# Second attention of a two-layer stack: from whole chunks of 128 tokens to two halves of 64 with a state between them

## What is computed

```python
def step(carry, qkv):
    S_K, C_QV, G = carry
    q_t, k_t, v_t = qkv
    C_prev = GAMMA * C_QV
    k_C = einsum('bhk,bhkv->bhv', k_t, C_prev)
    G = GAMMA * G + k_t[..., :, None] * k_C[..., None, :]
    S_K = GAMMA * S_K + k_t[..., :, None] * k_t[..., None, :]
    C_QV = C_prev + q_t[..., :, None] * v_t[..., None, :]
    S_C = einsum('bhij,bhjv->bhiv', S_K, C_QV)
    o_t = einsum('bhk,bhkv->bhv', q_t, S_C - G)
    return (S_K, C_QV, G), o_t
out = outs @ Wo
```

## Time and profile before

| what | value |
|---|---|
| median of 3 runs | 700.54 us |
| lowest, highest | 699.94, 701.98 us |
| span of the profiled execution, first to last instruction | 697.8 us |
| PE busy over the span | 640.0 us, 92% |
| DVE, ACT, POOL busy | 421.9, 301.7, 254.2 us |
| mean granted TensorE clock, share of full speed | 0.956 |

### The profile page before, as it was taken

The page is one execution under the profiler, slowest core; times in us unless marked ns, Lnnn a source line. Parts: engine busy times, 40 slices in busy tenths (PEclk is TensorE's granted clock), DMA queues, the critical chain, the costliest instruction groups (busy, mean ns, idle before and its releaser), DMA issues.

```text
span 697.8 us, 26323 instructions
## 1 busy us (share of the span) xinstructions
PE 640.0 (92%) x10918; PEld 545.8 (78%) x10918; DVE 421.9 (60%) x1384; ACT 301.7 (43%) x1017; POOL 254.2 (36%) x387
## 2 busy tenths in 40 slices
PE   5799999888759969999999999999997999999995
PEld 4466666666649957888888888888875899998995
DVE  3777677867534326577777686868674454444443
ACT  1556466543025404555545454545442353333231
POOL 2366566555620031122525252524242332232225
PEclk9789999998869989999999999999999899999999
DMA  7999000000048300000000000000401567676472
GB/s 195 310 323 268 22 3 3 2 10 17 24 137 243 87 26 7 8 8 8 20 11 18 16 15 15 16 20 8 156 15 24 170 208 233 215 232 227 144 241 61
DMA packets 50486, 65.68 MB, mean 94 GB/s; under 512 B 5169, under 2 KB 40209, under 8 KB 47425
## 3 DMA queue, kind: packets, MB, share of 16 engines
q1 hardware_dynamic: 44992, 57.22, 26.6%
q0 software_dynamic: 2912, 6.03, 2.6%
q10 hardware_dynamic: 2464, 0.76, 0.5%
HBM read 49.45 MB, written 18.87 MB: 98 GB/s over the span
## 4 chain that ended last, share of the span: by engine, by line
PE 58%; DVE 2%; another core or an unknown queue 1%; DMA 1%; issue 1%; ACT 0%; SPq 0%; DVEq 0%; PEldq 0%
PE bank L1903 6%; PE quad L1761 6%; PE quad L1885 6%; PE quad L1887 6%; PE bank L1786 4%; PE pair L1723 4%; PE bank L1809 3%; PE quad L1767 2%; PE pair L1724 2%; PE pair L1725 2%; PE bank L1819 2%; PE bank L1822 2%; PE pair L1748 2%; PE bank L1812 2%; PE bank L1905 1%; PE quad L1890 1%
## 5 line engine op out<-in xcount | busy, mean ns | idle before, releaser
L2159 DVE TENSOR_TENSOR h_masked<-quad,const 128x1536 f32<-128x1536 f32 (+2 forms) x66 | 112.7, 1707 | 63.6 <-PE quad L1767 54.4
L1997 ACT ACTIVATE f_sa<-quad 128x256 f32<-128x256 f32 (+1 forms) x115 | 40.1, 351 | 94.2 <-PE quad L1887 76.8
L2273 DVE TENSOR_TENSOR f_hid<-f_sa,quad 128x256 f32<-128x256 f32 (+1 forms) x115 | 43.0, 379 | 53.0 <-ACT f_sa L1997 52.2
L2377 POOL DMA_INDIRECT moe_slots<-g_pay,g_slot x28 | 28.9, 1031 | 77.3 <-PE bank L1831 68.8
L1885 PE MATMUL quad<-f_xT,wall 128*128 128x256 f32 (+1 forms) x190 | 51.5, 354 | 3.7 <-DVE f_hid L2273 3.6
L1903 PE MATMUL bank<-wall,f_hid 128*128 128x128 f32 x390 | 50.7, 277 | 1.1 <-DVE f_hid L2276 0.9
L1903 PEld LDWEIGHTS bank<-wall,f_hid 128*128 128x128 f32 x390 | 47.8, 192 | 3.7 <-DVE f_hid L2276 2.8
L1887 PE MATMUL quad<-f_xT,wall 128*128 128x256 f32 (+1 forms) x190 | 50.4, 347 | 0.0
L1761 PE MATMUL quad<-h_qk 32*128 32x128 f32 x1024 | 47.0, 298 | 0.0
L1974 ACT ACTIVATE h_gT<-bank 128x128 f32<-128x128 f32 x64 | 17.7, 277 | 66.1 <-PE bank L1812 66.1
L1761 PEld LDWEIGHTS quad<-h_qk 32*128 32x128 f32 x1024 | 34.7, 187 | 9.3 <-issue 7.4
(11 more groups left out here) (412 smaller groups left out, 1785.8 us busy)
## 6 DMA issues: line engine op xcount, KB each, us to landing
wall<-moe_w SPq DMA_DIRECT2D x23, 1088.0 KB, 5.2
moe_slots<-blank SPq DMA_DIRECT2D x2, 2112.0 KB, 25.9
wall<-in_experts_dram SPq DMA_DIRECT2D x1, 4120.0 KB, 22.1
e_w<-in_experts_dram SPq DMA_DIRECT2D x15, 257.5 KB, 3.1
moe_slots<-blank SPq DMA_DIRECT2D x1, 1984.0 KB, 9.8
moe_slots<-e_yg SPq DMA_DIRECT2D x7, 256.0 KB, 3.7
f_xg<-moe_slots SPq DMA_DIRECT2D x12, 132.0 KB, 4.6
moe_w<-in_moe_w_dram SPq DMA_DIRECT2D x1, 1408.0 KB, 7.2
```

Source lines behind the costliest of these rows:

```text
L1997: act.activation(sa[g % 3][:, 0:s], up_bank(n, f)[:, 0:s], ACT.Silu).then_inc(f_sa, 1)
L2159: dve.tensor_tensor(masked[k % 4][:, :, a * P:z * P], quad[:, :, a * P:z * P], cst("causal")[:, None, a * P:z * P].to_broadcast([P, HPG, ( ...
L2273: dve.tensor_tensor(hid[n % 2][:, f, 0:s], sa[g % 3][:, 0:s], up_bank(n, f)[:, T1:T1 + s], ALU.mult)\
L2377: pool.indirect_dma_start(out=t["moe1_slots"], out_offset=bass.IndirectOffsetOnAxis(ap=slot[:, b * 2 + k:b * 2 + k + 1], axis=0), in_=pay[ ...
```

## The change

Each unit is computed as two halves of 64 tokens. The scores of a half with itself are blocks of 64 x 64; the two halves of a unit stand beside one another as column tiles of the array (`tile_position=(h * D, r * S)`) and fill 64 columns of the moving operand each. The mask and the masked scores have 3 x 64 columns instead of 3 x 128. Between the halves stands a state, `mids`: VectorE adds the first half's contribution (a product that TensorE now makes in right) to the carried state. The products with the states then take the carried state for the first half and `mids` for the second. The chunk products come in two parts, `chunk_first` ahead of `from_states` and `chunk_second` behind it, each with row tiles of 64: one half of left beside the other half of right. State updates are now five groups of matmuls: two for the first half of unit now + 1 (k and v), two for the second half of unit now - 2, one for the first half of unit now - 1 (G). The copy to oT now also waits for the two additions that VectorE makes at the start of the next step.

The other hunks renumber the semaphores' starting counts, move the count of tokens (L1858) from left to token, and add waits for left and right at the end of the attention.

```diff
+HL_SUB = 64
...
-    parts["causal"] = np.concatenate([row <= col, row < col, row <= col], axis=1)
+    early, late = row % HL_SUB, np.arange(HL_SUB)[None, :]
+    parts["causal"] = np.concatenate([early <= late, early < late, early <= late], axis=1)
...
+    parts["decay_half"] = np.where(row < HL_SUB, 1.0, GAMMA ** P)
...
-masked = [sb(f"h_masked{k}", [P, HPG, 3 * P]) for k in range(4)]
+S = HL_SUB
+masked = [sb(f"h_masked{k}", [P, HPG, 3 * S]) for k in range(4)]
...
+mids = [sb(f"h_mid{k}", [P, 3 * D]) for k in range(4)]
...
-            pe.wait_ge(s_gc, now + 1)
+            pe.wait_ge(s_gc, now)
             last = pe.transpose(token[:, 2 * P:3 * P], gT[q][:, :], cst("ident"))
         if k % GROUPS == 2 and live(i, k, -3):
             q = unit(i, k, -3)[1]
-            pe.wait_ge(s_oc, now + 1)
+            pe.wait_ge(s_oc, now - 2)
+            if (i, k) == (CHUNKS - 1, PER + 2):
+                pe.wait_ge(s_tab, 1)
...
             for a in range(2):
-                for h in H:
-                    last = pe.matmul(quad[:, h, a * P:(a + 1) * P], qk[q][head(h), 1 - a, :],
-                                     qk[q][head(h), a, :], start=True, stop=True, tile_position=(h * D, 0))
+                for r in range(2):
+                    for h in H:
+                        last = pe.matmul(quad[half(r), h, a * S:(a + 1) * S], qk[q][head(h), 1 - a, half(r)],
+                                         qk[q][head(h), a, half(r)], start=True, stop=True,
+                                         tile_position=(h * D, r * S))
         if live(i, k, -1):
             q = unit(i, k, -1)[1]
-            pe.wait_ge(s_ac, now + 1)
-            for h in H:
-                last = pe.matmul(quad[:, h, 2 * P:3 * P], qk[q][head(h), 0, :], aT[q][head(h), :], start=True,
-                                 stop=True, tile_position=(h * D, 0))
+            pe.wait_ge(s_ac, now)
+            for r in range(2):
+                for h in H:
+                    last = pe.matmul(quad[half(r), h, 2 * S:3 * S], qk[q][head(h), 0, half(r)],
+                                     aT[q][head(h), half(r)], start=True, stop=True,
+                                     tile_position=(h * D, r * S))
...
-    def from_states(i, k):
+    def banks_free(i, k):
+
         now = i * PER + k
-        pe.wait_ge(s_gc, upto(now + 1, UNITS + 1))
-        pe.wait_ge(s_ac, upto(now + 1, UNITS + 1))
-        pe.wait_ge(s_oc, now + 1)
-        pe.wait_ge(s_st, upto(now + 6, UNITS))
+        if now == 0:
+            pe.wait_ge(s_midkv, 1)
+        if now > UNITS:
+            pe.wait_ge(s_midg, now - 1)
+        if now >= 3:
+            pe.wait_ge(s_oc, now - 2)
+            pe.wait_ge(s_st, upto(now - 2, LAST))
         m = routed(i, k, "slots")
         if m is not None:
             pe.wait_ge(r_place, m * 2 + 1)
         pe.nop(nofuse=True)
+
+    def chunk_left(i, k, r, part, first):
+
+        new = masked[(k - 1) % 4]
+        for h in H:
+            k_op = kg[k][half(r), 1, head(h)] if part else vt[k][half(r), head(h)]
+            last = pe.matmul(left[head(h), part * P + r * S:part * P + (r + 1) * S], k_op,
+                             new[half(r), h, 0:S] if part else new[half(r), h, S:2 * S], start=first,
+                             stop=True, tile_position=(r * S, h * D), skip_group_check=True)
+        return last
+
+    def chunk_right(i, k, r, part, first):
+
+        new, old = masked[(k - 1) % 4], masked[(k - 3) % 4]
+        q = unit(i, k, -2)[1]
+        for h in H:
+            k_op = kg[q][half(r), 0, head(h)] if part else vt[q][half(r), head(h)]
+            last = pe.matmul(right[head(beside(h)), half(r)], k_op,
+                             old[half(r), h, 0:S] if part else new[half(r), h, 2 * S:3 * S], start=first,
+                             stop=True, tile_position=(r * S, beside(h) * D), skip_group_check=True)
+        return last
+
+    def chunk_first(i, k):
+
+        for part in range(2):
+            if live(i, k, 0):
+                last = chunk_left(i, k, 0, part, part == 0)
+            if live(i, k, -2):
+                last = chunk_right(i, k, 1, part, part == 0)
+        if live(i, k, 0) or live(i, k, -2):
+            last.then_inc(s_first, 1)
+
+    def from_states(i, k):
+        now = i * PER + k
         q = unit(i, k, -2)[1]
         for part in range(2):
+            for r in range(2):
+                if live(i, k, 0):
+                    for h in H:
+                        of = mids[now % 4] if r else states[k]
+                        pe.matmul(left[head(h), part * P + r * S:part * P + (r + 1) * S],
+                                  of[head(h), D:2 * D] if part else of[head(h), 2 * D:3 * D],
+                                  qk[k][head(h), 1 - part, half(r)], start=False, stop=True,
+                                  tile_position=(h * D, h * D), skip_group_check=True)
+                if live(i, k, -2):
+                    for h in H:
+                        of = mids[(now - 2) % 4] if r else states[q]
+                        pe.matmul(right[head(beside(h)), half(r)],
+                                  of[head(h), 0:D] if part else of[head(h), 2 * D:3 * D],
+                                  qk[q][head(h), 0, half(r)] if part else aT[q][head(h), half(r)],
+                                  start=False, stop=True, tile_position=(h * D, beside(h) * D),
+                                  skip_group_check=True)
+
+    def chunk_second(i, k):
+
+        now = i * PER + k
+        last_left, last_right = None, None
+        near, far, done = live(i, k, 1), live(i, k, -1), live(i, k, -2, LAST)
+        if now >= 0:
+            pe.wait_ge(s_first, now + 1)
+        if near:
+            pe.wait_ge(s_kqt, (now + 3) * 2)
+        elif far:
+            pe.wait_ge(s_ng, now + 3)
+        pe.nop(nofuse=True)
+        for part in range(2):
             if live(i, k, 0):
-                for h in H:
-                    pe.matmul(left[head(h), part * P:(part + 1) * P],
-                              states[k][head(h), (0 if part else 2 * D):(D if part else 3 * D)],
-                              qk[k][head(h), 1 - part, :], start=(part == 0), stop=False,
-                              tile_position=(h * D, h * D), skip_group_check=True)
+                last_left = chunk_left(i, k, 1, part, False)
             if live(i, k, -2):
-                for h in H:
-                    pe.matmul(right[head(beside(h)), 0:P],
-                              states[q][head(h), (2 - part) * D:(3 - part) * D],
-                              qk[q][head(h), 0, :] if part else aT[q][head(h), :], start=(part == 0),
-                              stop=False, tile_position=(h * D, beside(h) * D), skip_group_check=True)
+                last_right = chunk_right(i, k, 0, part, False)
+        n, m, q = unit(i, k, 1)[1], unit(i, k, -1)[1], unit(i, k, -2)[1]
+        if near:
+            for h in H:
+                last_right = pe.matmul(right[head(h), P + D:P + 2 * D], kqt[n][half(0), 0, head(h)],
+                                       kg[n][half(0), 1, head(h)], start=not live(i, k, -2), stop=True,
+                                       tile_position=(0, h * D), skip_group_check=True)
+        if done:
+            for h in H:
+                last_left = pe.matmul(left[head(h), 2 * P:2 * P + 2 * D], kqt[q][half(1), 0, head(h)],
+                                      kg[q][half(1), :, head(h)], start=False, stop=True,
+                                      tile_position=(S, h * D), skip_group_check=True)
+        if near:
+            for h in H:
+                last_right = pe.matmul(right[head(h), P + 2 * D:P + 3 * D], kqt[n][half(0), 1, head(h)],
+                                       vt[n][half(0), head(h)], start=False, stop=True,
+                                       tile_position=(0, h * D), skip_group_check=True)
+        if done:
+            for h in H:
+                last_left = pe.matmul(left[head(h), 2 * P + 2 * D:2 * P + 3 * D], kqt[q][half(1), 1, head(h)],
+                                      vt[q][half(1), head(h)], start=False, stop=True,
+                                      tile_position=(S, h * D), skip_group_check=True)
+        if last_left is not None:
+            last_left.then_inc(s_left, 1)
+        if far:
+            if near:
+                pe.wait_ge(s_ng, now + 3)
+            for h in H:
+                last_right = pe.matmul(right[head(h), P:P + D], kqt[m][half(0), 0, head(h)],
+                                       kg[m][half(0), 0, head(h)], start=False, stop=True,
+                                       tile_position=(0, h * D), skip_group_check=True)
+        last_right.then_inc(s_right, 1)
...
-        if live(i, k, 0) or live(i, k, -2):
+        if live(i, k, 1) or live(i, k, 0) or live(i, k, -2):
+            banks_free(i, k)
+            chunk_first(i, k)
             from_states(i, k)
-            from_chunk(i, k)
+            chunk_second(i, k)
 
...
```

(43 more changed lines are left out.)

45 lines of the change are left out of this document (8 added, 37 removed).

## The result

The changed kernel takes 878.04 us as the median of 4 runs (875.95 to 880.5), the kernel before 700.24 us beside it. The ratio is 1.2535, with a 95% interval of 1.2501 to 1.2569. The forecast was 674 us. It is 204 us off and on the wrong side.

What follows compares the result with a forecast made beforehand. PE's matmul columns were taken to bound the kernel: -40 us from shorter steps, +13 for added waits and +0.5 for filling and emptying the pipeline gave -26.5, so 674 us, range 660 to 691.

Steps and rivals of the forecast that it cites:

- What bounds the kernel: Attention: PE bounds it, busy 262.37 of 264.20 us; a plain step of 3.85 us is explained by columns.
- PE, step by step: Plain step on PE: column savings less added costs give -0.63 us, a step of 3.22 us, -40 us over 64 steps.
- extra change of shape: PE going from chunk products to states and back to chunk products: one more change of tile shape, 0.14 us a step.
- rival (b): PE's steps: more is given back than counted, such as passes of many tiles held by issue; 687 us, chance 0.18.
- Rival (d): PE's small tiles: column or row tiles of 64 run one behind the other; +0.14 us a step, 710 us, chance 0.04.
- The other engines: DVE: mask falls to 0.95 us, two additions take 0.39 us, covered in a plain step; kqt's constant as column costs nothing.
- The wait that is added: Behind join, six chunks: PE waits 0.98 us at k = 2 and 1.07 us at k = 3, together 12.3 us.
- the sum: Whole kernel: -40 + 13 + 0.5 = -26.5 us, so 674.0 us.
- rival (c): PE starved of instructions: at 17.0 ns each, 450 make a step of 7.65 us, kernel 944 us; chance 0.04.
- The prediction's own sign for it: Plain steps on PE: gaps inside a run of small matmuls that nothing releases would show instruction starvation.
- The paragraph ahead of the rivals: A rule against the change: PE's 226 instructions a step become 450; by about 20 cycles each the step would nearly double.

Runs made afterwards that it cites:

- half the heads: The changed kernel with score, state, chunk and update products made for heads 0 and 2 of each group only: 694.07 us, ratio 0.988.
- one-pass products: The kernel before with v, kg, kqt and masked scores in bfloat16, one pass instead of two, at lower precision: 664.33 us, ratio 0.950.
- full_scores: The changed kernel with scores and mask as before, over all 128 columns, 48 instructions a step fewer: 834.1 us, ratio 1.191.
- after_bf16: The changed kernel with v, kg, kqt and masked scores in bfloat16, 104 instructions a step fewer: 778.39 us, ratio 1.110.

## Why the prediction was wrong, step by step

**What bounds the kernel** was read correctly for the kernel before, and stopped one question short. PE's columns did explain every start in the earlier trace rows. But a second limit stood just behind: at 18.5 ns an instruction the kernel before had only a sixth of slack to the rate of about 15.5.

**PE, step by step.** With all heads the plain step of 3.22 us does not exist, not even between the stops. Passes of 64 columns do share the array: eight tiles of left and right lie in one pass, and the passes of L1804 (413.18, 413.26, 413.32) follow one another at 0.08 and 0.06 us. But the whole step, put together from stretches at full clock in which PE is not stopped, is as long as before. In PE's timeline of the changed kernel:

```profile
413.18 0.26 PE L1804 MATMUL bank<-h_masked,h_vt 64*32 64x64 f32 x4
...
413.26 0.24 PE L1804 MATMUL bank<-h_masked,h_vt 64*32 64x64 f32 x4
...
413.32 0.24 PE L1804 MATMUL bank<-h_masked,h_kg 64*32 64x64 f32 x4
...
413.57 0.26 PE L1838 MATMUL bank<-h_qk,h_state 32*32 32x64 f32 x4
...
415.56 0.28 PE L1871 MATMUL bank<-h_kg,h_kqt 64*32 64x32 f32 x6
...
416.07 0.49 PE L1729 MATMUL pair<-hT_all,hla_wq 128*128 128x128 f32 x2
```

```profile
503.14 0.49 PE L1729 MATMUL pair<-hT_all,hla_wq 128*128 128x128 f32 x2
...
504.33 0.49 PE L1770 MATMUL quad<-h_qk 32*64 32x64 f32 x32
504.62 0.49 PE L1778 MATMUL quad<-h_aT,h_qk 32*64 32x64 f32 x16
505.04 0.26 PE L1804 MATMUL bank<-h_masked,h_vt 64*32 64x64 f32 x4
...
506.28 0.26 PE L1838 MATMUL bank<-h_qk,h_state 32*32 32x64 f32 x4
...
507.07 0.26 PE L1804 MATMUL bank<-h_masked,h_vt 64*32 64x64 f32 x4
...
507.36 0.28 PE L1871 MATMUL bank<-h_kg,h_kqt 64*32 64x32 f32 x6
```

| part of a plain step, us | before | forecast | changed kernel, not stopped |
|---|---|---|---|
| to the scores | 1.19 | 1.19 | 1.19 |
| scores | 0.88 | 0.50 | 0.71 |
| chunk products, both parts | 0.89 | 0.59 | 0.68 |
| products with states | 0.60 | 0.60 | 0.79 |
| updates | 0.29 | 0.34 | 0.51 |
| sum | 3.85 | 3.22 | 3.88 |

(The forecast's extra change of shape, 0.14, stands with the chunk products.) Over the whole attention the medians of such stretches add up to 3.87 us. The prediction charged for columns and not for the number of products. With half the heads, the same passes and 216 instructions fewer, the step is 3.15 us; the 0.73 us between are 3.4 ns for each of these instructions. That is rival (b)'s "pass of many tiles held by its issue", at 0.66 us a step where it had 0.2. As an estimate from these rows, without any stop the change would have gained nothing: 700 + 64 x 0.03 = 702 us, and the added waits on top. Rival (d) falls, as passes of 64 columns were not 0.11 us apart. The step had to be put together from parts, since each step of 450 instructions holds the end of at least one block.

**The other engines.** The mask was put at 0.95 us and takes 0.96 in the median, 0.93 on average. The two additions were put at 0.39 us together; the rows are from the kernel with half the heads, which has all of VectorE's work. Not foreseen: kqt's copy takes 0.48 us with its constant as a column, where it took 0.39; no run shows that this reached the path. Timeline of DVE at the head of step k = 3, of ACT in a plain step:

```profile
439.41 0.60 DVE L2112 TENSOR_SCALAR p_xn<-x_sb,p_mv,p_rstd 128x128 f32<-128x128 f32 x2 [1.76 <-POOL p_rstd L2422]
439.93 0.21 DVE L2212 TENSOR_TENSOR h_mid<-h_state,bank 128x64 f32<-128x64 f32 x1
440.06 0.18 DVE L2216 TENSOR_TENSOR h_mid<-h_state,bank 128x32 f32<-128x32 f32 x1
440.16 0.28 DVE L2221 TENSOR_TENSOR h_aT<-bank,const 128x128 f32<-128x128 f32 x1
```

```profile
431.23 0.48 ACT L2034 ACTIVATE h_kqt<-pair,const 128x256 f32<-128x256 f32 x1
```

**The wait that is added.** Forecast: 0.98 us at k = 2 before Wo's product and 1.07 at k = 3 before the second scores, in six chunks. Shown, with half the heads: both, six times each, with the releasers named. The longest are 0.76 and 0.83 us, and together they are 8.2 us (3.2 and 5.0) where 12.3 was forecast. The mechanism was right and the size half as large again as measured, and in the changed kernel itself the waits vanish behind the stops. In PE's timeline of the kernel with half the heads:

```profile
434.96 1.16 PE L1756 MATMUL pair<-hla_wo,h_oT 128*128 128x128 f32 x8 [0.76 <-ACT h_oT L2057]
...
440.49 0.34 PE L1778 MATMUL quad<-h_aT,h_qk 32*64 32x64 f32 x8 [0.83 <-DVE h_aT L2221]
```

**The step that failed** is the sum, which charged columns and waits and put the number of instructions at nothing; its rival (c), starvation, had a chance of 0.04 and decided. The rival was named, with its place, its price and the count of 450 instructions. The prediction's own sign for it, gaps inside a run of small matmuls that nothing releases, is what the trace shows. Two things were wrong in it. First its chance: I set it by the earlier trace rows, 64 instructions within 0.32 us, and that is a stretch much shorter than a block of 256. The paragraph ahead of the rivals said that 450 instructions a step are no burst, and the chance then used the burst as the evidence. The limit is one on the average over a block: the changed kernel can run a block at 6.4 ns an instruction, nearly as fast as those rows, and it is then held. Second its size: 17.0 ns was the average of a plain step that was not starved, so 944 us was an upper end. With 15.5 ns, 450 instructions make a step of 7.0 us. As an estimate that is 64 x (7.0 - 3.85) = 202 us more if every step were plain. Steps with Wo or rank were longer before and hold few more instructions, so they grow less; 178 was measured.

The Trainium skill, Runtime: NRT & Kernel Launch, Instruction fetch mechanics, has both halves of this. It states blocks of 16 KiB, 256 instructions, which the stops here show exactly. It also says that fetching is hidden behind a floor of about 20 cycles an instruction. Here it is not hidden: a block runs off at 6.4 ns an instruction and PE stops at its end. The prediction weighed that floor and left the block out, and it was the other way round.

**A part of the loss is the clock.** The granted clock over the attention fell from 0.99 to 0.83: 143 of the 425 us were at the lower of its two levels, 1.2 GHz, against 7 of 256 before. It fell 25 times within the attention, each time less than 4 us after the start of a stop of 1.4 us or more. How much that cost can be estimated from the blocks: 55 of the 107 ran wholly at the upper level and took 3.70 us each on average (1.21 of it stopped), 12 ran wholly at the lower one and took 4.29 (0.25 stopped), the 40 mixed ones 4.08. With 3.70 for all, the attention would be 22 us shorter. So most of what the slower passes cost is taken out of the stops, and the clock is a small part of the 178 us by this estimate.

## What to carry to other kernels

Cutting a product into smaller ones that lie beside one another saves columns and costs instructions, and both have a price. The halves were to save 0.77 us a step of columns with 224 more instructions, 3.4 ns each. Here one instruction costs 15 ns in a starved stretch, and even between the stops about the 3.4 ns that it was to save. Before such a change, divide the time of the stage by the instructions of its busiest engine, over stretches of several hundred instructions and never over a burst, and ask how far the new quotient falls; this kernel had about a sixth to go. If the quotient is the limit, look for versions with fewer instructions for the same columns: one-pass products gained 35 us where halves lost 178.

## What the runs showed of the hardware

- TensorE stopped at the end of a block of 256 of its instructions, in the middle of equal products: 76 of the 77 stops in the changed kernel. Over the attention, four kernels with 21203 to 27410 instructions had 15.5 to 16.1 ns each.
- These stops hung on the transfer of a block: every one of the 76 ended 1.2 to 1.6 us after such a transfer had ended. The transfers came one at a time, 0.9 to 1.4 us each, and began in the median 1.2 us after a block had been begun. Their queue has about 1% of the DMA engines' time, so the bytes are not what limits; blocks came one after the other. What the time around a transfer is spent on stays open; no run varied it.
- The price showed in the difference of two versions as well: 14.3 ns an instruction (full_scores), 15.0 (after_bf16).
- In stretches without a stop the products had a price of their own: 3.88 us, put together from its parts, for a step of 450 instructions, 3.15 us for one of 234 with the same passes.
- 14418 instructions in 247.8 us, 17.2 ns each, still had stops by "issue" of up to 1.3 us in the kernel with half the heads, 6.5 us together, as a plain step of 3.15 us has 13.5 ns for each of its 234. Its granted clock was 0.94, with 30 us at the lower level against 7 before. Both are part of why that kernel gained only 7 us on the kernel before; how much each cost was not separated.
- An ACT copy of 256 columns took 0.48 us with its scale as a column of SBUF and 0.39 us with a constant.
